# Cross-attention and a routed feed-forward layer: router logits as four column tiles, copied by ScalarE, then added and turned by a second product

## What is computed

```python
x = x + xattn(layernorm(x), ctx, ...)      # softmax(q k' / sqrt(32)) v, projections with biases
y = layernorm(x)
logits = (y / |y|) @ c_norm.T + y @ w_route.T      # c_norm: centroids of length 1; 8 experts
gates = softmax over the two largest logits
x = x + sum over experts of gates * (gelu(y @ w1 + b1) @ w2 + b2)
```

## Time and profile before

| | |
|---|---|
| median of 3 runs | 1539.64 us (1538.95, 1539.64, 1547.55) |
| span of the profiled execution | 1544.8 us |
| PE busy | 1453.1 us, 94% |
| POOL, DVE, ACT busy | 70%, 64%, 55% |
| mean granted clock of PE | 0.967 |

### The profile page before, as it was taken

One profiled execution on the slowest core, in us unless ns is written; L12 is line 12 of the kernel. 1 busy time (PEld: TensorE's weight loads), 2 busy tenths in 40 slices (PEclk: granted clock), 3 DMA queues, 4 the chain that ended last, 5 costly groups with the idle time before them and its releaser, 6 DMA issues.

```text
span 1544.8 us, 34359 instructions
## 1 busy us (share of the span) xinstructions
PE 1453.1 (94%) x11588; PEld 1139.7 (74%) x11588; DVE 994.5 (64%) x1423; ACT 849.7 (55%) x1807; POOL 1074.5 (70%) x917
## 2 busy tenths in 40 slices
PE   3899999999999999999999999999999687999997
PEld 3667777777777777777777777777777455989896
DVE  5576757676767676767666676667676567444443
ACT  4456555565555565656565655555555362555554
POOL 3367777777777777777777777777777642766775
PEclk9999999999999999999999999999999777999999
DMA  5444444454536363535454535353535473777785
GB/s 180 123 108 127 129 132 135 125 142 117 158 101 174 95 172 100 168 101 161 108 156 114 163 97 163 104 164 107 160 95 146 124 270 49 138 142 130 144 142 85
DMA packets 134953, 206.75 MB, mean 134 GB/s; under 512 B 33808, under 2 KB 70832, under 8 KB 134656
## 3 DMA queue, kind: packets, MB, share of 16 engines
q1 hardware_dynamic: 120544, 173.20, 40.9%
q0 software_dynamic: 14240, 31.35, 11.3%
HBM read 64.29 MB, written 38.66 MB: 67 GB/s over the span
## 4 chain that ended last, share of the span: by engine, by line
PE 79%; POOL 8%; DVE 4%; ACT 4%; issue 3%; DMA 1%; SPq 1%; POOLq 0%; ACTq 0%; DVEq 0%
PE M L379 12%; PE S L1725 11%; PE M L381 11%; PE M L380 11%; PE O L1741 9%; POOL psum_p L583 6%; PE M L1702 4%; ACT pr L867 2%; PE M L1759 2%; PE M L1976 2%; PE M L1995 2%; PE M L1977 2%; PE M L1978 2%; PE M L1996 2%; PE M L1997 2%
## 5 line engine op out<-in xcount | busy, mean ns | idle before, releaser
L583 POOL TENSOR_TENSOR psum_p<-psum_p,pr 125x896 f32<-125x896 f32 x254 | 536.5, 2112 | 153.0 <-ACT pr L867 130.3
L867 ACT ACTIVATE pr<-S 125x448 f32<-125x448 f32 x768 | 385.1, 540 | 173.2 <-PE S L1725 157.0
L1170 DVE TENSOR_REDUCE mx_parts<-M 112x2 f32<-112x1024 f32 x256 | 302.7, 1220 | 106.2 <-PE M L1702 106.2
L1725 PEld LDWEIGHTS S<-qst,kst 128*125 128x125 f32 x1536 | 223.7, 189 | 109.8 <-ACT pr L867 57.1
L1725 PE MATMUL S<-qst,kst 128*125 128x224 f32 x1536 | 285.7, 293 | 14.2 <-ACT pr L867 12.4
L580 POOL TENSOR_TENSOR psum_p<-pr 125x896 f32<-125x896 f32 x64 | 135.0, 2109 | 132.4 <-ACT pr L867 132.4
L1741 PE MATMUL O<-pr,v 125*32 125x224 f32 x3072 | 184.0, 361 | 1.9 <-ACT pr L867 1.9
L1174 DVE TENSOR_REDUCE mx_parts<-M 112x4 f32<-112x952 f32 x128 | 141.2, 1145 | 64.0 <-PE M L1702 64.0
L835 ACT ACTIVATE kh_s<-M,bk_s 128x376 fp32r<-128x376 f32 (+1 forms) x128 | 73.5, 574 | 190.9 <-PE M L381 190.9
L379 PE MATMUL M<-ctx_h,wk_h 128*128 128x376 f32 (+1 forms) x384 | 139.6, 364 | 1.0 <-DVE ql_s L1149 0.6
L380 PE MATMUL M<-ctx_l,wk_h 128*128 128x376 f32 (+1 forms) x384 | 132.7, 346 | 0.0
(11 more groups left out here) (253 smaller groups left out, 3042.4 us busy)
## 6 DMA issues: line engine op xcount, KB each, us to landing
kst<-kh_s SPq DMA_DIRECT2D x512, 93.8 KB, 2.3
kst<-kl_s SPq DMA_DIRECT2D x256, 93.8 KB, 2.2
ctx_r<-ctxT SPq DMA_DIRECT2D x48, 375.0 KB, 4.2
qst<-qh_s SPq DMA_DIRECT2D x128, 112.0 KB, 3.0
rows_d<-x_res SPq DMA_DIRECT2D x32, 448.0 KB, 4.3
w_l<-w SPq DMA_DIRECT2D x16, 512.0 KB, 7.9
x_ln<-x SPq DMA_DIRECT2D x17, 448.0 KB, 4.7
q_own<-qh_s SPq DMA_DIRECT2D x256, 28.0 KB, 1.9
```

What stands on the lines that cost most here:

```text
L583: pool.tensor_tensor(out=total, in0=total, in1=tiles[half], op=ALU.add).then_inc(sum_step, 1)
L867: act.activation(pr[0:KP, (3 * g + p) % 2, j, :, :], S[0:KP, n % SB, 0:2 * NQ].rearrange("p (i n) -> p i n", i=2), ACT.Exp).then_inc(exp_d ...
L1170: dve.tensor_reduce(mx_parts[0:QP, pair, u, 0:1], M[0:QP, pair, 0:FIRST_KEYS], AX.X, ALU.max).then_inc(max_done, 1)
L1725: last = pe.matmul(S[0:KP, n % SB, NQ * h:NQ * (h + 1)], kst[:, i, j, o:o + KP], qst[:, i, j, :], start=True, stop=True)
```

## The change

The logits of one batch are made in two steps.

1. `logits(b)`: the weights are `rw`'s piece c, widened from 16 to 32 columns by zeros, and the moving data are all 224 columns of `y_T`'s piece c. The four pieces go to four column tiles: 32 partitions each of one bank ("lgs", bank 4), so that there are four products of 224 columns, each complete in itself and not added to the others.
2. ACT copies the bank to `lg_parts` (`keep_parts`, between exponentials 9 and 10, ahead of `max_out`).
3. `turn_logits(b)`: for each half of the rows, `lg_parts`' 112 columns are the weights and `pick` (128 x 16: four identity matrices of 16 below each other, with gaps of zeros) is the moving data. This adds the four pieces and turns the result to rows by experts, both halves into one bank ("lg", bank 1), as `lg0` and `lg1` had it.

The turning of the maxima uses bank 4 after "lgs", and `turn_logits` stands behind it, as the last of `first`. DVE's `keep_logits` reads the same numbers as before, from one bank; it has moved behind `o_lo`. Set-up: one memset for `rw`'s zero columns and one reduction for `pick` on DVE; the starting waits ask for five constants in place of three. `y_T`'s copies of batch 14 are no longer held back until the last group is over. SP's code is written as functions; `stack_k` is two functions in the same order, of which the first no longer waits for the low halves' banks. `mneg` and `rw` change their places in SBUF.

```diff
-                      ("den", g - 1, 1), ("K1", g + 2, 0), ("V5", b, 4), ("X2", g + 1, None), ("lg0", b - 2, 4),
-                      ("lg1", b - 2, 1), ("mT", g + 1, 4)]
+                      ("den", g - 1, 1), ("K1", g + 2, 0), ("V5", b, 4), ("X2", g + 1, None), ("lgs", b - 2, 4),
+                      ("mT", g + 1, 4), ("lg", b - 2, 1)]
...
+                def keep_parts(b):
+                    if not 0 <= b < B:
+                        return
+                    wait_full(act, "lgs", b)
+                    if b:
+                        wait_full(act, "lg", b - 1)
+                    act.activation(lg_parts[:, :], bank_of("lgs", b)[:, 0:NQ], ACT.Copy).then_inc(freed("lgs", b), 1)
...
-                def yT_part(b, i, g=GROUPS):
-                    if not 0 <= b < B or g == GROUPS - 1:
+                def yT_part(b, i):
+                    if not 0 <= b < B:
...
                     exps(g, 9)
+                    keep_parts(b - 2)
                     max_out(g + 1)
...
+                dve.memset(rw[:, :, 2 * E:HD], 0.0).then_inc(consts, 1)
...
+                dve.tensor_reduce(pick[:, :], id_s[:, :].rearrange("p (c n) -> p n c", n=HD)[:, 0:2 * E, :], AX.X,
+                                  ALU.add).then_inc(consts, 1)
...
                     top(g + 1)
+                    o_lo(g - 1)
                     keep_logits(b - 2, 0)
                     keep_logits(b - 2, 1)
-                    o_lo(g - 1)
...
-                def logits(b, qt):
+                def logits(b):
...
                     for c in range(DC):
-                        last = pe.matmul(out[0:QP, 0:2 * E], y_T[:, c, QP * qt:QP * (qt + 1)], rw[:, c, :],
-                                         start=c == 0, stop=c == DC - 1)
+                        last = pe.matmul(out[HD * c:HD * (c + 1), 0:NQ], rw[:, c, :], y_T[:, c, :], start=True, stop=True)
+                    last.then_inc(full, 1)
+
+                def turn_logits(b):
+                    if not 0 <= b < B:
+                        return
+                    out, full = claim("lg", b)
+                    wait_free(pe, "lgs", b)
+                    for qt in range(QT):
+                        last = pe.matmul(out[0:QP, 2 * E * qt:2 * E * (qt + 1)], lg_parts[:, QP * qt:QP * (qt + 1)],
+                                         pick[:, :], start=True, stop=True)
                     last.then_inc(full, 1)
...
                     score(g, 9)
-                    logits(b - 2, 0)
-                    logits(b - 2, 1)
+                    logits(b - 2)
                     score(g, 10)
                     score(g, 11)
                     transpose_max(g + 1)
+                    turn_logits(b - 2)
```

More of the change, by code:

```diff
@@ L68 @@
 OS = 5
+CONSTS = 5
 MAXIMA = ("X0", "X1", "X2")
@@ L185, in expert_phase @@
         psum_p = sb("psum_p", [P, 2, GH, NQ])
-        zone_c = here[0] = here[0] + 2 * (GH - 1) * NQ * 4
+        after_sums = here[0]
+        mneg = sb("mneg", [GH * QT, QP], F32R)
+        here[0] = after_sums + 864
+        lg_parts, pick = sb("lg_parts", [P, NQ]), sb("pick", [P, 2 * E])
+        zone_c = here[0] = after_sums + 2 * (GH - 1) * NQ * 4
         wo_h, wo_l = sb("wo_h", [P, DC, D], F32R), sb("wo_l", [P, DC, D], F32R)
@@ L417, in load_res, with load_next_x, load_next_res, load_next_ctx @@
                     sp.dma_start(x_res[0:QP, :, :], xv[b]).then_inc(res_in, 16)
+                def load_next_x(b):
+                    if b < B:
+                        load_x(b)
+                def load_next_res(b):
+                    if 1 <= b < B - 1:
+                        load_res(b)
+                def load_next_ctx(b):
+                    if b < B:
+                        for c in range(CC):
+                            load_ctx(b, c)
                 def store_x1(b):
@@ L449, in stack_k, with stack_k_low @@
                     sp.wait_ge(kh_done, 2 * (g + 1))
+                    if g >= 2:
+                        sp.wait_ge(s_full, 12 * (g - 1))
+                    for row in (0, 2 * HD):
+                        for j in range(GH):
+                            sp.dma_start(kst[row:row + HD, i, j, :].bitcast(F32),
+                                         kh_s[HD * j:HD * (j + 1), i, :].bitcast(F32)).then_inc(kst_in[i], 16)
+                def stack_k_low(g):
+                    if not 0 <= g < GROUPS:
+                        return
+                    i = g % 2
                     wait_free(sp, "K0", g)
@@ L453, in stack_k @@
                         sp.wait_ge(s_full, 12 * (g - 1))
[L454 to L457, removed]
+                    for j in range(GH):
+                        sp.dma_start(kst[HD:2 * HD, i, j, :].bitcast(F32),
+                                     kl_s[HD * j:HD * (j + 1), i, :].bitcast(F32)).then_inc(kst_in[i], 16)
                 def spread_q(g):
@@ L496, in load_pieces, with before @@
                         sp.dma_start(lo.bitcast(F32), src).then_inc(ew_in[n], 16)
-                for g in range(-2, GROUPS + LAST):
-                    t, b = g % NG, g // NG
+                def before(g):
                     if g == GROUPS - NG:
@@ L512, in _, with after @@
                         load_pieces(E + 2, 2 * E)
[L513 to L541, removed]
+                def after(g):
                     if g == GROUPS - 2:
@@ L544, in _, with first, second, third @@
                         load_pieces(0, E)
+                def first(g, b):
+                    stack_k_high(g + 1)
+                    stack_k_low(g + 1)
+                    spread_q(g + 2)
+                    load_next_res(b - 1)
+                    stack_q(g + 1)
+                    put_max(g + 1)
+                def second(g, b):
+                    stack_k_high(g + 1)
+                    stack_k_low(g + 1)
+                    stack_q(g + 1)
+                    spread_q(g + 2)
+                    put_max(g + 1)
+                def third(g, b):
+                    stack_q(g + 1)
+                    load_next_x(b + 2)
+                    stack_k_high(g + 1)
+                    stack_k_low(g + 1)
+                    spread_q(g + 2)
+                    put_max(g + 1)
+                    store_x1(b - 1)
+                def fourth(g, b):
+                    stack_k_high(g + 1)
+                    stack_k_low(g + 1)
+                    load_next_ctx(b + 2)
+                    spread_q(g + 2)
+                    stack_q(g + 1)
+                    put_max(g + 1)
+                    store_xn(b - 1)
+                for g in range(-2, GROUPS + LAST):
+                    before(g)
+                    (first, second, third, fourth)[g % NG](g, g // NG)
+                    after(g)
                 wait_full(sp, "O1", B - 1)
```

74 lines of the change are left out of this document (37 added, 37 removed).

## The result

The changed kernel is slower: 1564.38 us (median of 4 runs, 1559.74 to 1564.8) against 1541.24 for the kernel before (4 runs, 1538.95 to 1547.55). The ratio is 1.0142, with a 95% interval of 1.0109 to 1.0174; the time lies above the forecast range. The profiled execution took 1564.51 with a span of 1562.7. A time is thus its span and 1.8 us more, so the profiled execution of before was one of about 1546.6, among its slower ones, and not of 1544.8, as I had taken it.

What follows compares the result with a forecast made beforehand. PE's queue was taken to bound the kernel (busy 94% of the span). Terms 3.9 + 0.6 + 1.1 + 0.2 = +5.8 us gave 1550.6 or 1545.4; the forecast was the middle, 1548, range 1534 to 1556.

Steps and rivals of the forecast that it cites:

- PE's own work: Logits in each batch: 1.0 us of PE's queue for 1.5, 0.5 us a batch less, 7 us in 14 batches.
- X0 0.57 us later: End of `first`: X0 waits for DVE's reads of both logits halves and comes 0.57 us later in each batch.
- my walk: Step-by-step timing of group 40 from the logits to X0, putting X0 at 816.61 where it was 816.04.
- my bound of 0.8: Upper bound on X0's lateness per batch, if each hand-over costs another 0.05 us; the lower bound was 0.3.
- The clock (mean batch 75.1): Batches of 74.2 us without a clock fall, 75.6 with one; mean near 75.1, +3.9 us over 13 batches.
- 9 in 14: Share of batches expected to be hit by a clock fall, each fall costing 1.4 us.
- The ends (+1.9): Terms outside the 13 batches: 0.6 for the 14th place, 1.1 for the last batch, 0.2 at the start.
- The start and the 14th place: DVE's reduction for `pick` at the start, +0.2 us; the 14th place with logits in full company, +0.6.
- batch 14's `y_T` copies: Copies now between exponentials of the last group, whose end POOL's sums set: 0, at most 0.5 us.
- the last logits: Group 68: ACT's copy stands behind `y_apply`; corrections end 2.2 us later, 1.1 hidden by `rest_part`, 1.1 showing.
- the third, a fall in each batch and a stall of 0.8: Chance 13 in 100: every batch has a clock fall and X0's stall is 0.8 us; +16 us, 1555.6 to 1561.
- The second, in which X0 isn't late: Chance 6 in 100: DVE reads both halves by 815.7, PE's saving shows and falls go; -21 us, 1519.

Runs made afterwards that it cites:

- e2_early: Changed kernel with logits ahead of score 9, turn_logits behind score 10, second values behind that, DVE's logits reads ahead of o_lo: 1526.84 us, ratio 0.9909.
- e9_before_early: Kernel before, without column tiles, its 16 logits products moved ahead of score 9 and the second half of the values behind it: 1528.27 us, ratio 0.9938.
- e10_olo_late: Changed kernel with o_lo moved into the next group, behind k_lo of the second keys, away from POOL's additions: 1556.62 us, ratio 1.0097.
- e1_order: Changed kernel with DVE's reads of the logits back ahead of o_lo: 1607.86 us, ratio 1.0434.
- e4_before_swap: Kernel before with only o_lo moved ahead of keep_logits, the changed kernel's DVE order without column tiles: 1556.7 us in a single run.
- e6_hold: Changed kernel with two last-batch edits undone: batch 14's y_T copies held until the last group is over, last y_apply behind last keep_parts: 1559.09 us, ratio 1.0141.
- e7_best: e2_early and e6_hold together, except that the last y_apply stands behind exponential 9: 1520.76 us, ratio 0.9881.
- e5_filler: Changed kernel with eight unused products of 224 columns in PE's wait ahead of X0: 1547.32 us, ratio 1.003.
- e3_swap_banks: Changed kernel with two banks exchanged: turn_logits writes bank 4, the turning of the maxima bank 1: 1536.93 us in a single run, beside 1544.03 for before.

## Why the prediction was wrong

The sum of the prediction was +5.8 us, and the spans give +17.9. Of the 12.1 that it missed, 8.6 are in the batches between groups 8 and 60 (the late X0 and the clock) and 3.5 at the ends.

**PE's own work (0.5 us a batch less)**: right. The logits take 0.51 to the next score (816.19 to 816.70), and where nothing waits the batch is 0.66 shorter (e2_early against e9_before_early).

**X0 0.57 us later**: the mechanism was right, its size was not, and here is the first step that failed. I wrote that exponentials 10 and 11 come earlier, "and DVE's `o_lo` too; neither is waited for there". DVE's reads do wait for `o_lo`: the change puts it ahead of them and to a time at which POOL adds. It cost 0.40 of the late X0 (817.93 for 818.33; e10_olo_late gives 0.40 at X0 and 0.43 a batch back). Without it (e10_olo_late) X0 comes 3.22 behind score 9, for 2.75 before and 3.32 in my walk, as the turning of the maxima is 0.1 earlier than there; and a batch is only 74.02 - 73.67 = 0.35 longer, since about 0.1 is taken back between X0 and the next score 9, which I had ruled out. With it X0 is 0.87 late against score 9, beyond my bound of 0.8, and 0.78 of this is left in the batch.

In the earlier trace rows `o_lo` took 0.44 only because it stood at the joint of two POOL additions: the second starts at 815.62 and `o_lo` at 815.64, and there it was POOL that was held, whose two additions (L599) together took 2.84 us where they take 2.52 in e1_order (688.59). The trace of before has other instances of `o_lo` of 1.9 and 2.17 us, and I hadn't looked at them.

What they show is that `o_lo`, whose two tensors both lie in SBUF, ends 0.2 to 0.3 us after the end of a POOL addition (in the changed kernel the one that ran when it started, in e1_order the third), while `keep_logits` and `k_lo`, which read one tensor from PSUM, keep their duration beside the same additions. The page "SBUF — State Buffer" of the Trainium skill, section "SBUF: two separate sides", has the rule: a VectorE instruction with two SBUF inputs and a GpSimd instruction that reads SBUF lock each other out of a shared port pair for a whole instruction, whoever is first. The traces here agree that one of the two is held (`o_lo` 2.17 for 0.44, or POOL 2.84 for 2.52). They don't fix who goes first: at 815.62 POOL is recorded 0.02 ahead and still `o_lo` was not held, and in e1_order `o_lo` waited through three additions and not one.

**The clock (mean batch 75.1)**: that the falls would stay, but not in each batch, was right, and the "9 in 14" too: nine of the 13 batches have one. The failed step is that each fall costs one unit: three of the nine were twice as long, so a batch was on the mean 75.76 = 984.9 / 13. Against the +3.9 of this term it was +12.5 from turning to turning: 13 x 0.21 = 2.7 of the difference is the later X0 (0.78 for 0.57), and the other 5.9 are 17.0 us of falls, where I had 13 x 0.86 = 11.2. In e10_olo_late, with 0.40 less idle time, all nine falls are single; in e4_before_swap and e6_hold, with X0 as late as in the changed kernel, three of nine are double again. That the doubles come from the longer wait is argued from these, not shown.

**The ends (+1.9)**: wrong; they came to +5.4 (17.9 less the 12.5 from turning to turning). The start and the 14th place came to -0.4 for my +0.8. For batch 14's `y_T` copies I had "0, at most 0.5": e6_hold wins 0.9 at the first w_h by taking them and the later edit back. For the last logits I had 1.1 beyond what is hidden: the two edits together cost 3.4 at the sum over the choices (90.5 for 87.0), so about 2.5 are due to the last logits. The 2.2 us that I gave for the lateness (its terms add to 2.1) were too few: PE waits 3.75 for ACT's copy there and runs at half clock. The last 1.9, in the experts, I can't lay to the change. From the first gather to the end took 249.1 us before and 251.0 after; the nine other kernels, with the same code there, took 245.2 to 252.7.

**The rivals**: the third, a fall in each batch and a stall of 0.8, had the right stall and came nearest (to 1561). It was given 13 in 100 since I held 0.8 to be the end of the bounds. The second, in which X0 isn't late, gave 21 us less than before. e2_early removes the lateness by an earlier place and is the fair comparison: 23.9 us less between groups 8 and 60 (948.5 for 972.4), where the rival had 22.4, and 17 less in the median. That e7_best ran at 1520.76, near the rival's 1519, is luck in part, as it also takes back two edits that the rival kept. The guess that the 8.6 us between the runs of before are clock falls is borne out: in 16 runs of before on one chip, from 1530.02 to 1547.13, the mean granted clock goes from 0.974 in the shortest to 0.962 in the longest, and the runs of a kernel without falls between groups 8 and 60 lie within 2.9 to 6.7 us (e2_early, e5_filler, e7_best, e9_before_early).

**What stays open**: why the falls vanish in e3_swap_banks, whose X0 (0.86 behind the turning) is between that of before (0.42, with 11 falls) and of e10_olo_late (1.75, with nine). How late X0 is doesn't decide it alone: before has the least late X0 of the three, but its 16 thin records of the logits stand just ahead, and e9_before_early, which moves only these and the values, has no fall. That move changes both what stands ahead of X0 and how long PE waits for it, and no run parts the two.

## What to carry to other kernels

A part that does less work on the engine that sets the time can lose if its result is read right ahead of that engine's next buffer: place the producer so early that the reads lie beside other products (here 37 us between the spans of the changed kernel and of e2_early, which do the same work), or give it a bank that is wanted a little later (e3_swap_banks). When an instruction is moved, look at all its instances in the trace, not at the one beside the change: a minimum of 0.44 with a maximum of 2.17 says that its duration depends on its neighbour. And read the engine's busy time after a change that left its work alone: DVE's +22 us was the first trace of the cause.

## What the runs showed of the hardware

- `o_lo` (128 x 224 fp32, both tensors in SBUF) took 0.44 us alone, 2.17 beside one POOL addition and 4.31 across three. POOL's next instruction can go ahead of the held one: in e1_order POOL passed from L638 to L622 (691.07) while DVE had been waiting since 689.08. It need not: in the changed kernel `o_lo` got in behind the addition that ended at 818.16, and it was POOL's next one (818.12) that took 1.42 us for 1.27.
- Eight products without use in a wait of PE's made the changed kernel faster (ratio 1.003 to before, for 1.0142), by holding the granted clock at 1.00 over 967 us, where it was 0.98 in 985.
- A low stretch in the clock (granted 0.50 for 3.4 us) costs 1.4 us a batch (75.87 for 74.45), and one of twice the length 2.9 (77.3).
- Entering 32-column tiles of fp32 products cost 0.1 us: the logits start 0.41 us behind score 9 (816.19 for 815.78), where they started 0.31 behind it in the kernel before (813.60 for 813.29). Eight records of 224 columns took 0.51 to the next score.
